# Layer 0 attention: softmax sums of two key tiles, added by VectorE before TensorE sums them

## The reference

```python
h = _layernorm(x) * (1 + ca) + sa
q, k, v = heads(h @ Wq.T, 16), heads(h @ Wk.T, 4), heads(h @ Wv.T, 4)
scores = einsum('bhqd,bhkd->bhqk', q, repeat(k, 4)) * 64 ** -0.5 + causal
probs = softmax(scores)
x = x + ga * (heads_back(einsum('bhqk,bhkd->bhqd', probs, v)) @ Wo.T)
```

## Time and profile before

| | |
|---|---|
| median of 3 runs | 1538.77 us (1535.51 to 1541.72) |
| profiled execution | 1542.66 us, span 1540.9 us |
| busy in the span: PE, DVE, ACT, POOL | 1315.5, 973.5, 693.4, 115.4 us |
| layer 0's attention | about 44 to 672 us |
| mean granted clock of TensorE | 0.905 |

### The profile page before, as it was taken

How to read it: one execution, slowest core, us unless ns; L and a number is a source line. 1 busy time by engine, 2 the same in 40 slices (tenths; PEclk the granted TensorE clock), 3 DMA queues, 4 the chain that set the end, 5 groups by cost and what they waited for, 6 DMA issues and landing times. The chain is left out here.

```text
span 1540.9 us, 21422 instructions
## 1 busy us (share of the span) xinstructions
PE 1315.5 (85%) x7772; PEld 775.7 (50%) x7772; DVE 973.5 (63%) x1750; ACT 693.4 (45%) x1319; POOL 115.4 (7%) x155
## 2 busy tenths in 40 slices
PE   4688999999999999967999977415898988889998
PEld 3344444454544444445888865312343433256886
DVE  4555464545545454157999984735777775257998
ACT  2232434242524343434666655411466665425664
POOL 0000000000000001000000000201011111010000
PEclk9798999999999999978999987855899998768998
DMA  3101112020201020104766620023233220102220
GB/s 102 40 15 34 31 32 43 23 47 15 48 18 43 15 43 15 29 2 98 159 148 146 158 60 1 1 47 90 46 58 61 50 47 20 42 21 78 75 102 28
DMA packets 51875, 82.14 MB, mean 53 GB/s; under 512 B 17020, under 2 KB 34724, under 8 KB 47844
## 3 DMA queue, kind: packets, MB, share of 16 engines
q1 hardware_dynamic: 50412, 76.78, 21.5%
q10 hardware_dynamic: 1376, 4.20, 1.1%
HBM read 63.75 MB, written 6.20 MB: 45 GB/s over the span
## 5 line engine op out<-in xcount | busy, mean ns | idle before, releaser
L621 DVE TENSOR_REDUCE mraw<-ps 128x1 f32<-128x512 f32 (+3 forms) x304 | 192.8, 660 | 129.5 <-PE ps L507 73.2
L1325 PE MATMUL ps<-qA 128*128 128x512 f32 x960 | 251.8, 399 | 14.5 <-POOL qA L1435 10.8
L723 ACT ACTIVATE shared<-ps 128x512 f32<-128x512 f32 (+1 forms) x216 | 119.4, 567 | 261.4 <-PE ps L540 259.9
L1046 DVE TENSOR_REDUCE mraw<-ps 128x2 f32<-128x1024 f32 (+3 forms) x160 | 173.8, 1114 | 81.9 <-PE ps L954 57.3
L1325 PEld LDWEIGHTS ps<-qA 128*128 128x128 f32 x960 | 181.6, 192 | 62.5 <-POOL qA L1435 12.5
L1111 ACT ACTIVATE shared<-ps 128x512 f32<-128x512 f32 (+2 forms) x320 | 154.1, 561 | 112.2 <-PE ps L970 111.8
L539 PE MATMUL ps<-qA,kH 128*128 128x512 f32 (+3 forms) x384 | 167.6, 447 | 5.8 <-DMA qB<-mT 5.8
L501 PE MATMUL ps<-kH,qA 128*128 128x512 f32 (+3 forms) x384 | 137.3, 411 | 34.8 <-DVE qA L611 18.5
L1389 ACT CAST qA<-shared 128x512 fp32r<-128x512 f32 x160 | 99.3, 621 | 90.2 <-DVE shared L1527 88.8
L1337 PE MATMUL ps<-qA,kH 128*128 128x512 f32 x480 | 136.1, 392 | 4.1 <-DVE qA L1451 4.1
L540 PE MATMUL ps<-qB,kL 65*128 65x512 f32 (+3 forms) x384 | 132.7, 356 | 0.0
(11 more groups left out here) (247 smaller groups left out, 1750.1 us busy)
## 6 DMA issues: line engine op xcount, KB each, us to landing
shared<-comb SPq DMA_DIRECT2D x92, 256.0 KB, 4.4
qB<-qA SPq DMA_DIRECT2D x16, 512.0 KB, 4.8
rB<-a0rec_dram SPq DMA_DIRECT2D x60, 128.0 KB, 3.0
shared<-comb SPq DMA_DIRECT2D x7, 1024.0 KB, 4.5
rB<-a1rec_dram SPq DMA_DIRECT2D x28, 128.0 KB, 2.7
e0wUp<-in_w SPq DMA_DIRECT2D x48, 64.0 KB, 4.5
qA<-q_split SPq DMA_DIRECT2D x24, 128.0 KB, 4.1
q_split<-qA ACTq DMA_DIRECT2D x4, 512.0 KB
```

Of the source, the lines that this page charges most:

```text
L621: nc.vector.tensor_reduce(out[:, h0:h0 + n_h, qt % 4], src, AX, ALU.max).then_inc(w_free, 1)
L723: nc.scalar.activation(probs(n)[:, hs[0]:hs[-1] + 1, lo:512], src, ACT.Exp, scale=scale)\
L1046: nc.vector.tensor_reduce(out[:, :, js[0]:js[-1] + 1, qt % 4], src, AX, ALU.max).then_inc(x_free, 1)
L1325: ins = nc.tensor.matmul(bank[0:M, :], w[par][:, at:at + M], h[:, cols], start=(r == 0), stop=(r == 2))
```

## The change

Four pairs of neighbouring units of a group, (0, 1), (4, 5), (6, 7) and (8, 9), are paired; the last group leaves (8, 9) alone. For a pair DVE adds the two probability tiles in fp32 into a tile PAIR, which lies in the residual's buffer, and PE multiplies only PAIR with ones: one quad instead of two. Off the diagonal there is one add of 512 per head, in the step of the second unit (after the first, second and third head's exponential) and at the head of the next step. On the diagonal an "edge" copy takes the 128 queries that only the first unit has, and two "both" adds take two heads each, 384 queries wide, one step later. PE's quad on PAIR (`pair_sums`) stands ahead of the values of the step that closes the pair. PAIR is single: the adds of a pair wait (`pv_done`) until PE has read the pair before. ACT also waits for the adds before it overwrites a tile. SP reloads x from HBM near the end of the stage, and a semaphore of the experts' stage is replaced by one of the layer norm's.

```diff
+    PAIRS = [n for n in range(STEPS) if n % NU in (0, 4, 6, 8) and n != NU * (G - 1) + 8]
+    closing = {n + (3 if on_diagonal(n) else 2): n for n in PAIRS}
+    paired = {n + i for n in PAIRS for i in range(2)}
+    for n in PAIRS:
+        if on_diagonal(n):
+            adds.setdefault((n + 1, 3), []).append((n, "edge", 0))
+            adds.setdefault((n + 2, 0), []).append((n, "both", 0))
+            adds.setdefault((n + 2, 1), []).append((n, "both", 2))
+        else:
+            for h in range(3):
+                adds.setdefault((n + 1, h + 1), []).append((n, "head", h))
+            adds.setdefault((n + 2, 0), []).append((n, "head", 3))
...
+        PAIR = k.x[:, :, :].rearrange("p t d -> p (t d)").rearrange("p (h q) -> p h q", h=REP)
+        closed_by = {n: m - LAG for m, n in closing.items()}
...
+                def pair_sums(n):
+                    opened(n)
+                    lo = unit_lo(n)
+                    pe.wait_ge(paired_up, added(n))
+                    for h in range(REP):
+                        nc.tensor.matmul(SUMS[CT * h:CT * (h + 1), lo:512], k.ones[:, 0:CT], PAIR[:, h, lo:512],
+                                         start=(UNITS[n % NU][1] == 0), stop=False, skip_group_check=True)
...
-                    for h in range(REP):
+                    for h in range(0 if n in paired else REP):
                         ins = nc.tensor.matmul(SUMS[CT * h:CT * (h + 1), lo:512], k.ones[:, 0:CT],
...
+                    if n in closing:
+                        pair_sums(closing[n])
                     if n >= LAG:
                         values(n - LAG)
...
+                def add(n, what, h):
+                    lo = unit_lo(n)
+                    at = PAIRS.index(n)
+                    if at and what != "both":
+                        dve.wait_ge(pv_done, closed_by[PAIRS[at - 1]] + 1)
+                    if what == "head":
+                        dve.wait_ge(p_done, first_score[n + 1] + h + 1)
+                        ins = nc.vector.tensor_tensor(PAIR[:, h, :], probs(n)[:, h, :], probs(n + 1)[:, h, :], ALU.add)
+                    elif what == "edge":
+                        dve.wait_ge(masked, diagonals[n + 1])
+                        ins = nc.vector.tensor_copy(PAIR[:, :, lo:lo + P], probs(n)[:, :, lo:lo + P])
+                    else:
+                        dve.wait_ge(masked, diagonals[n + 2])
+                        hs = slice(h, h + 2)
+                        ins = nc.vector.tensor_tensor(PAIR[:, hs, lo + P:512], probs(n)[:, hs, lo + P:512],
+                                                      probs(n + 1)[:, hs, lo + P:512], ALU.add)
+                    ins.then_inc(paired_up, 1)
...
-                    for idx in due.get(n, []):
-                        take(idx)
+                    for at, (hs, fills) in enumerate(parts(n)):
+                        for one in adds.get((n, at), []):
+                            add(*one)
+                        for idx in fills:
+                            take(idx)
...
                         act.wait_ge(pv_done, n - RING + 1)
+                        if n - RING in paired:
+                            act.wait_ge(paired_up, added(n - RING))
...
+                    if n == NU * (G - 1) + 10:
+                        sp.wait_ge(pv_done, closed_by[PAIRS[-1]] + 1)
+                        sp.dma_start(k.x[:, :, :], x.rearrange("b (t p) d -> p (b t) d", p=P))\
+                            .then_inc(x_ld, 16)
+                sp.wait_ge(x_ld, 16)
```

More of the change, by code:

```diff
@@ L346, in _, with stage_attention64 @@
                 rms_deviation(3)
-def stage_attention64(nc, k, name, hT, wqk, wo, y):
+def stage_attention64(nc, k, name, hT, wqk, wo, y, x):
     G = NKV * B
@@ L449, in parts @@
         return [(hs, fills[size * i:size * (i + 1)]) for i, hs in enumerate(heads)]
+    PAIRS = [n for n in range(STEPS) if n % NU in (0, 4, 6, 8) and n != NU * (G - 1) + 8]
+    closing = {n + (3 if on_diagonal(n) else 2): n for n in PAIRS}
+    paired = {n + i for n in PAIRS for i in range(2)}
+    adds = {}
+    for n in PAIRS:
[7 more added lines that the diff above has]
+            adds.setdefault((n + 2, 0), []).append((n, "head", 3))
     with ExitStack() as c:
         sem = lambda n: c.enter_context(nc.semaphore(name + n))
+        paired_up, x_ld = sem("paired_up"), sem("x_ld")
+        added = lambda n: 3 * sum(m <= n and on_diagonal(m) for m in PAIRS) + \
+            4 * sum(m <= n and not on_diagonal(m) for m in PAIRS)
         w_full, w_free, q_hi, folded = sem("w_full"), sem("w_free"), sem("q_hi"), sem("folded")
@@ L542, in scores, with opened @@
                     ins.then_inc(s_full, 1)
+                def opened(n):
+                    g, (qc, kt) = n // NU, UNITS[n % NU]
+                    if kt == 0 and n:
+                        pe.wait_ge(o_act, 2 * g + qc)
+                        pe.wait_ge(o_dve, 2 * g + qc)
+                def pair_sums(n):
[5 more added lines that the diff above has]
+                                         start=(UNITS[n % NU][1] == 0), stop=False, skip_group_check=True)
                 def values(n):
@@ L551, in values @@
                         pe.wait_ge(p_done, first_score[n + 1])
-                    if kt == 0 and n:
-                        pe.wait_ge(o_act, 2 * g + qc)
-                        pe.wait_ge(o_dve, 2 * g + qc)
+                    opened(n)
                     lo = unit_lo(n)
@@ L561, in values @@
                                 v = k.V[:, b * TPB + kt, kv * hd + half * CT:kv * hd + (half + 1) * CT]
-                                nc.tensor.matmul(O[p][CT * at:CT * (at + 1), lo:512], v,
+                                ins = nc.tensor.matmul(O[p][CT * at:CT * (at + 1), lo:512], v,
                                                  probs(n)[:, 2 * p + i, lo:512], start=first, stop=last,
                                                  skip_group_check=True)
-                    for h in range(REP):
+                    for h in range(0 if n in paired else REP):
                         ins = nc.tensor.matmul(SUMS[CT * h:CT * (h + 1), lo:512], k.ones[:, 0:CT],
@@ L1237, in stage_experts @@
         CE, logits = choose.E, choose.logits
-        scored, weights, turned, copied, stored, rows_full, rows_taken, links = (
-            sem(n) for n in ("scored", "weights", "turned", "copied", "stored", "rows_full", "rows_taken", "links"))
+        scored, weights, turned, copied, stored, rows_full, rows_taken = (
+            sem(n) for n in ("scored", "weights", "turned", "copied", "stored", "rows_full", "rows_taken"))
+        links = k.ln_sems[0]
         score, comb = (k.oU_flat[:, i * NT * CE:(i + 1) * NT * CE].rearrange("p (t e) -> p t e", t=NT)
@@ L1459, in low_part @@
                         .then_inc(h_low, 1)
-                n_links = [0]
+                n_links = [k.ln_links]
                 def link(ins):
@@ L1541, in _ @@
                         finish(dve, ch, acc(ch))
+                k.ln_links = n_links[0]
 def stage_linear(nc, k, hT, y):
@@ L2074, in program @@
         stage_ln(nc, k, "n0", k.hT, m0(1), m0(0), tiles=(k.wv0[:, :], 256, store_v))
-        stage_attention64(nc, k, "a0", k.hT, a["wqk0"], a["wo0"], k.y)
+        stage_attention64(nc, k, "a0", k.hT, a["wqk0"], a["wo0"], k.y, a["x"])
         def scale_y(act, ch):
```

## The result

The changed kernel takes 1554.2 us (median of 4 runs, 1550.0 to 1560.6) against 1538.2 before; the ratio is 1.0114 (95% interval 1.0076 to 1.0153). Timed again with 12 runs it is 1551.8 against 1538.0, ratio 1.0089 (1.006 to 1.0119). It is slower by 16 and by 14 us, 0.6% to 1.5%. The prediction was 1542 with a range to 1553, and it called "within 0.5%" the likeliest. Both the size and the side of the 0.5% were missed. The profiled execution of the changed kernel is its longest of the four (1560.6 us).

A forecast was written before the change was run, and what follows sets the result against it. PE bounds the attention on average, DVE steps 5 and 6. Saved quads against stalls gave -4.8 us, the clock +8.3: +3.5 on the profiled 1542.66, so 1546.2; that execution lies 3.9 above the median, hence 1542, range 1529 to 1553.

The forecast's parts named there:

- What bounds the stage: Attention: PE bounds it on the average, but DVE has no gap in steps 5 and 6, where PE waits for maxima.
- The adds: DVE, attention: slots of 0.62 us per head's add, 0.87 per "both" add, 0.5 per edge copy; some 74 us in all.
- Step 6: Steady groups: adds delay the maximum that PE's third job needs, +1.6 us a group, with 2.8 us of idle.
- The step-7 term: Step 7 of a steady group: two adds ahead of the fifth maximum delay PE's seventh job by 0.9 us.
- what a quad is worth: PE, attention: a removed wide sums quad saves 0.97 us, net 3.46 a group and 26.9 over eight groups.
- The ends: First group: stalls 5.5 less 3.46 saved, +2.0 us; last group, without maxima: -2.7, with 0.1 back.
- The clock: Step 6's idle brings a second half-rate stretch in each of six groups, 1.3 us each; +8.3 with the first group's 0.5.
- Rival A: Attention: the clock does not fall a second time, since PE works between step 6's stalls; -4.8 us, 1534, chance 0.24.
- Rival B: Attention: DVE takes the adds without holding PE; up to -26.9 us, 1512, or about 1523 with half the stalls; chance 0.12.
- Rival C: Steps 6 and 7: the low clock comes twice in a group, +7.8 us over six groups, 1550; chance 0.22.
- The copy-out of step 2: Step 2: the edge copy delays the copy-out that the group's first value matmul waits for, +0.25 us a steady group.
- The edits costed at nothing: ACT's and PE's new waits, the residual's reload, the renamed semaphore and colliding selects and adds: no time on the path.

The follow-up runs named there:

- y1: The changed kernel with only pair (4, 5) of each group: 1551.7 us, ratio 1.0131 to the kernel before.
- y2: The changed kernel without pair (4, 5), the other pairs kept: 1531.5 us, ratio 0.9972 to the kernel before.
- x3: The changed kernel without DVE's adds and the waits for them, PE's fewer quads kept: 1515.0 us, ratio 0.9889 to the kernel before.
- y3: The changed kernel with the next scores' first matmul run six times in step 6's stall: 1540.0 us, ratio 1.0027 to the kernel before.
- w1: The changed kernel, unaltered, traced a third time in a single execution: attention 607.0 us, rest 935.4, 36.8 at half rate.
- x4: The changed kernel with all adds made, but PE summing every unit as before: 1574.0 us, ratio 1.0243 to the kernel before.
- x2: The changed kernel with no pairs, only the residual's reload and the exchanged semaphore kept: 1538.2 us, ratio 1.0009 to the kernel before.
- z2: The kernel before with the next scores' first matmul run seven times in step 4's stall of six steady groups: 1532.1 us, ratio 0.9964.

## Why the prediction was wrong, point by point

**What bounds the stage: right.** PE bounds it on the average, DVE bounds steps 5 and 6, and the third job of step 6 was where the change would show. `y1` and `y2` bear it out.

**The adds: right.** A head's add takes 0.68 us and a slot of 0.60 (I took 0.62); a "both" add 0.95, or 1.13 in the mean where POOL's selects meet it; the edge copy 0.42, or 0.68 in the six of fifteen that start inside a select, for my 0.5. DVE's busy time in the whole kernel grew by 70.6 us for the 74 predicted.

**Step 6: the length right, the idle time too large.** The walk of DVE's queue said 1.6 later, with the half rate costing 1.3 on top, 2.9 in all. Measured in the steady group shown: step 5 grows by 0.37, for which I had nothing, and step 6 by 2.57, 1.4 of it waits and 1.2 half rate. The 2.8 us of idle that I put into step 6 counted the second job's 0.5 twice, for the third job's 1.66 contains it. Of the 4.65 us ahead of the fall 1.80 are idle, less than step 4's 1.92 and not more. The step-7 term (0.9 of stall for 0.97 saved) came out at -0.01 for the predicted -0.07.

**The term that was mis-sized: what a quad is worth.** I priced it at 0.97 us, the distance from the start of a sums quad to the next scores, and took 26.9 us off PE. What goes when the quad goes is less: in the timeline after, a value block followed by scores takes 359.84 to 361.67, 1.83 us (1.86 elsewhere), where it took 351.75 to 353.49, 1.74, with the quad behind it. I read the 0.1 us as the change from 32-column to 128-column products, which falls to whatever block comes last, so a removed quad gives 0.85 to 0.88. The change takes 31 quads off in all, so by that price the PE half is 23 to 24 us, and `x3` measured 23 timed and 21 in its trace without the clock's share. That is 3 to 4 us of the error, and step 5's 0.37 in each group is 2 more. Both are part of what the groups without any half rate show: 0.2 us longer than before, where I had 0.7 shorter, 5 us over six groups. The ends fit no better: up to the first step-4 stall of the steady groups the changed kernel takes 2.1 us more, with the clock, for my 2.5, and the last group is 1.0 shorter in the traces of before and after, not 2.6. My sum for the attention was +3.5, with the quad's price alone it would be +7; the traces show 6.5, so a clock term that was too large covered part of what the sum lacked.

**The clock: right in kind, the size partly by luck.** I took 8.3 us, from a second low stretch in each of six groups at 1.3 each. The stretch came in 9 of 24 groups, in one of the four traces in none, and four times it was double. By the length of the groups a single one costs 0.6 to 0.8 and a double one 2.3 to 2.4: with five single and four double ones in 24 groups that is 0.5 us a group, 3 us in six where I had 7.8. The total half-rate time gives 7 over four traces (14 us more, half of it lost); the steady groups don't hold all of it, and the stretches elsewhere make the total come near. My reason for the fall, more idle time than step 4's, did not hold either, and the same stall was followed by it or not. Without the clock's share the attention is 584.5 in the mean of the four against 585.2, about level, where I had -4.8. With step 6's stall filled (`y3`) the attention is as long as without pairs. Rival A (no second fall, 1534) had its condition met in `w1`, but its time not: that execution's attention is 607.0, 1.6 longer than without pairs and not 4.8 shorter. Rival B (DVE takes the adds for nothing) is ruled out by `x4`. Rival C (two low stretches a group, 1550) is nearest in time, and its condition, a second stretch right behind the first, was met in four of 24 groups.

**The copy-out of step 2: right in kind, 0.45 for 0.25.** It is a small part.

**The edits costed at nothing: right.** `x2` shows it for the reload. The rule on the shared lock held as it was put: POOL's busy time rose from 115.4 to 126.9 us, since selects and adds block each other. No wait of PE is for a select. DVE waited 3.9 us for selects, which I had not counted, in front of the first "both" add of (8, 9).

**What failed, in one line:** the saving on PE, 26.9 us for 23 to 24, made the attention 4.8 us shorter without the clock, where it is about level, and no step of the prediction had the 7 us outside the attention, whose cause stays open. A range that goes only by the changed stage, in a kernel whose single runs spread by 10 us and more, was too narrow on top.

## What to carry to other kernels

A stall of the matmul engine is priced twice: its own length, and the half-rate stretch that can follow it, in step 6 1.4 us and, where it follows, 1.2 more. Whether it follows differs between groups and executions of one kernel, so one trace does not price it. If a stall can't be removed, repeating harmless matmuls in it keeps the rate (0.4% for the kernel before, 10 to 12 us for the changed one). Work moved to a half-empty engine belongs into the gaps of its timeline, counted with everything that stands in them: the same idea cost 14 us in one place and gave 16 in another (there with three pairs fewer). And the price of a removed block is measured from a neighbour that already lacks it, not from the block's own duration.

## What the runs showed of the hardware that I had not expected

After 1.43 us of idle in step 6, with 0.30 us and less around it, the granted clock fell from 2.4 to 1.2 GHz in 9 of 24 steady groups of the changed kernel and not in the other 15; in the kernel before, with 0.80 us in pieces at the same place, it had not the earlier trace rows. With six matmuls in the 1.43 us it did not fall there. In `z2` 0.32 us of the 1.92 were left idle and the mean clock was 1.00 over five groups.

The edge copy of 512 fp32 elements within SBUF takes 417 ns in the last row below and an add of as many 681. Of the eight edge copies from `shared`, six start inside a select of POOL and take 0.68 us, the other two 0.42. In the changed kernel's groups (mean ns):

```profile
L688 DVE TENSOR_TENSOR x_res<-shared,rB 128x512 f32<-128x512 f32 x32 | 21.6, 681 | 0.0
L695 DVE TENSOR_TENSOR x_res<-shared 128x768 f32<-128x768 f32 x16 | 18.0, 1131 | 0.0
L695 DVE TENSOR_TENSOR x_res<-rB,shared 128x768 f32<-128x768 f32 x14 | 13.3, 952 | 3.9 <-POOL shared L799 3.9
L691 DVE COPY x_res<-rB 128x512 f32<-128x512 f32 x7 | 2.9, 417 | 0.0
```

By the Trainium skill ("VectorE: DVE Perf Modes", section "The perf-mode tier table") an fp32 copy within SBUF runs at twice an add's rate. The trace agrees in the direction: here the copy is 1.6 times as fast. The second and third rows differ by 0.18 us on one shape: the second "both" add of pair (0, 1) meets POOL's select in seven of eight groups and takes 1.38 us for 0.95; such a select takes up to 1.93 us for 0.64. The Trainium skill ("SBUF — State Buffer", section "SBUF: two separate sides") says that a VectorE instruction with two SBUF inputs and a GpSimd instruction take turns; the trace agrees, with these numbers.
